# A four-layer graph network: node tiles kept in the order of their edge counts, source rows relabelled on VectorE

## The chip, the cores and the metric

The kernel runs on one core of one Trainium2 chip, as one launch. The metric is the device time of the launch in microseconds (us), smaller being better.

## The reference

A graph has 6250 nodes with 128 features each and 100,000 edges (`src`, `dst`, sorted by `dst`). Four layers are applied, each to `relu(layernorm(x))` and added to `x`:

```python
x = x + L0(h)   # continuous filters: per edge x[dst] * fsum(edge_weight), summed at src; two dense products
x = x + L1(h)   # two graph attention layers, 1 head: softmax over the edges of dst, sum of h[src]
x = x + L2(h)   # per edge MLP on [x[src], edge_attr, global], mean at dst, MLP on the nodes
x = x + L3(h)   # graph attention, 8 heads
```

Layers 1 to 3 gather a row of each edge's source node and sum at the destination node. Layer 0 reads the row of the destination node and sums at the source node. Nothing in the result depends on the order in which nodes or edges are stored, but output row i must be node i.

## The kernel before

Nodes are held on chip in 49 tiles of 128 (the last has 106), which is dimension `b` of `X`, `ACC`, `H`. Edges are sorted into slots, 128 to an edge tile. An edge tile of the regular part (733 tiles, `REG`) holds edges of one destination node tile alone; what is left over, some 49 tiles (`ZT`), lies in "the zone", where an edge tile may touch several node tiles. Eight edge tiles make a half: 92 regular halves and 13 zone halves (`IH`), the latter placed between the regular ones by a table (`Order`; in layer 0 after the halves 5, 10, ..., 65).

**Setup** (L275 to 1034). VectorE counts the edges of each node tile, finds for each node tile where its edges begin (L806 to 827, 21 small instructions in a row, each of which waits for the one before), and then computes a slot for each edge, chunk by chunk of columns (`slot_round`, `slot_rows`). As chunks become ready, GpSimd (POOL) scatters the records (64 attributes and 5 fields) to `edge_records` in DRAM with 782 indirect DMAs (L559), 28 to a round, and ScalarE copies each round's fields and indices (L721, L723). SyncE (SP) loads `x` near the start (L438, L439); VectorE waits for it at L1011, late in setup. ScalarE serves the square root of the first layer norm (L743) only after the copies of round 25.

**Layer 0, destination pass** (`layer0_dst_pass`, L1531 to 1776). For each half:
- VectorE makes one-hot rows (`prepare`, L1611, L1612, one-hot L1451), waiting first for the DMA that stores the one-hots of two halves before;
- TensorE turns them (`turn`, L1717), ScalarE copies them out of PSUM (L1751, L1752), TensorE multiplies them with the rows of `H` (`pick`, L1729);
- VectorE (`finish_regular`) waits until the ring buffer of four halves before has been scattered (L1637, L1639), then for the product, and scales it (L1643, two instructions, in the trace one row "x2");
- POOL scatters the eight tiles to `layer_messages` with eight indirect DMAs (L1765). After half 72 it also scatters the 49 tiles of the zone (L1772).

The order on VectorE is: prepare half k+1, finish half k, prepare half k+2, and so on. The order on TensorE is: turn k+1, pick k, turn k+2, pick k+1. So between two finishes lie, one after the other, VectorE's prepare, TensorE's turn and TensorE's pick. A zone half has a prepare, a turn and a pick of its own but gives POOL nothing to scatter. SP stores the one-hots and the turned ones for the later layers (L1578, L1581) and loads the next half's records (L1572). The record fields of all regular halves stay on chip (`fields`); after the last half two casts (L1703, L1704) make `src_ix`, the gather indices of layers 1 to 3, out of them.

**Layers 1 to 3** each store a table of node rows and gather from it with indirect DMAs on POOL (L1929, eight per half, and 49 for the zone), with TensorE, VectorE and ScalarE working on the halves behind. The destination tile of each edge tile is read from a table (`acc_of_d`, `tile_of_d`, `acc_of_s`) into registers (TENSOR_LOAD, L1458, L1465).

**Output** (L2648 to 2673). VectorE finishes `X` in four parts of 12, 12, 12 and 14 node tiles, and SP writes each part with one DMA (L2670), and the 106 rows of the last tile with another (L2672).

Of the kernel before, what the change touches and what calls it, by code (L numbers as in the profile page):

```python
# [19 lines left out]
I32 = mybir.dt.int32  # L20
# [124 lines left out]
def gnn(nc, a, out):  # L145
# [30 lines left out]
    with ctx:  # L176
# [15 lines left out]
        tile_of_i = sb("tile_of_i", [1, IH * G], I32)  # L192
        adc = sb("adc", [P, NBP * 48], BF16)
# [80 lines left out]

        def setup():  # L275
# [56 lines left out]
            upto = [tb([P, NB2]) for q in range(3)]  # L332
            upto_col = [tb([64, 1]) for q in range(3)]
            edges_upto, before_zone = tb([P, NB2]), tb([P, NB2 + 1])
            zone_from, zone_shift = tb([P, NB2]), tb([P, NB2])
# [19 lines left out]
            with stage_of_work():  # L355
# [19 lines left out]
                masked_ready, slots_summed = sem("masked_ready"), sem("slots_summed")  # L375
                filt_ready, cos_ready, upto_ready, upto_turned, reached_ready, tiles_counted = (
# [28 lines left out]
                with nc.Block() as block:  # L405
                    @block.sync
                    def _(sp):
# [70 lines left out]
                    def _(pool):  # L478
# [17 lines left out]
                        for t in bias_row:  # L496
                            st.then(pool.memset(t[:, D:D + 2], 0.0))
                        pool.sem_inc(consts, 1)
# [74 lines left out]
                    def _(pe):  # L573
# [18 lines left out]
                        for q in range(2):  # L592
                            nc.tensor.matmul(bank[q][:, 0:NB2], tri[0:EP, :], count[q], start=True, stop=True)
                            nc.tensor.matmul(bank[2 + q][:, 0:NB2], ones[0:EP, :], count[q], start=True,
                                             stop=True).then_inc(offs_in_psum, 1)
                        for f in range(FILTERS_AHEAD, NF):
                            add_filter(f)

                        pe.wait_ge(weights_in, 16 * NW)
                        for n, (w, lo, hi) in enumerate(((wm1, 0, 128), (wm1, 128, 192), (wm1, 192, 256))):  # L600
# [7 lines left out]
                        for c in range(1, CHUNKS):  # L608
                            for i in range(NB2):
# [21 lines left out]
                        for q in range(3):  # L631
# [3 lines left out]
                        for q in range(2):  # L635
                            pe.wait_ge(reached_ready, q + 1)
                            for n in range(2):
                                nc.tensor.matmul(bank[2 + n][:, 0:NTP // 2], ones[0:NODE_TILES, :],
                                                 reached[0:NODE_TILES, n * (NTP // 2):(n + 1) * (NTP // 2)],
                                                 start=True, stop=True).then_inc(tiles_counted, 1)  # L640
# [106 lines left out]
                    def _(dve):  # L747
# [58 lines left out]
                        dve.wait_ge(offs_in_psum, 2)  # L806
                        st.then(v.tensor_copy(ntile[0], bank[2][:, 0:NB2]))
                        st.then(v.tensor_scalar(ntile_i[1], bank[3][:, 0:NB2], float(2 * P - 1), None, ALU.add))
                        st.then(v.tensor_copy(ntile_i[0], ntile[0]))
                        st.then(v.tensor_tensor_scan(edges_upto, ntile[0], ntile[0], 0.0, ALU.add, ALU.bypass))  # L810
                        st.then(v.tensor_single_scalar(ntile_i[0], ntile_i[0], 7, ALU.logical_shift_right))
                        st.then(v.tensor_single_scalar(ntile_i[1], ntile_i[1], 8, ALU.logical_shift_right))
                        st.then(v.tensor_tensor(zone_shift, edges_upto, ntile[0], ALU.subtract))
                        st.then(v.tensor_copy(ntile[0], ntile_i[0]))
                        st.then(v.tensor_scalar(ntile[1], ntile_i[1], 2.0, None, ALU.mult))
                        st.then(v.tensor_tensor_scan(upto[0], ntile[0], ntile[0], 0.0, ALU.add, ALU.bypass))
                        st.then(v.tensor_tensor_scan(upto[1], ntile[1], ntile[1], 0.0, ALU.add, ALU.bypass))
                        st.then(v.memset(before_zone[:, 0:1], 0.0))
                        st.then(v.tensor_scalar(upto[0], upto[0], float(REG), None, ALU.min))
                        st.then(v.tensor_tensor(ntile[1], upto[1], ntile[1], ALU.subtract))  # L820
                        st.then(v.tensor_scalar(before_zone[:, 1:NB2 + 1], upto[0], float(P), None, ALU.mult))
                        st.then(v.tensor_scalar(ntile[1], ntile[1], float(P), -1.0, ALU.mult, ALU.add))
                        st.then(v.tensor_copy(zone_from, before_zone[:, 1:NB2 + 1]))
                        st.then(v.scalar_tensor_tensor(off[0], before_zone[:, 0:NB2], -1.0, bank[0][:, 0:NB2], ALU.add, ALU.add))
                        st.then(v.tensor_tensor(off[1], ntile[1], bank[1][:, 0:NB2], ALU.add))
                        st.then(v.tensor_tensor(zone_shift, zone_shift, before_zone[:, 0:NB2], ALU.subtract))
                        st.then(v.scalar_tensor_tensor(zone_shift, zone_shift, float(ZONE_AT * P), zone_from, ALU.add, ALU.subtract))
# [107 lines left out]
                        for c in range(1, CHUNKS):  # L935
                            for i in range(NB2 // 2):
                                slot_round(i, c, loop_c, (c - 1) * (NB2 * 6) + i * 12, False)
                            slot_rows(c, Steps(dve, chunk_steps, c * 13 - 13).then)
                        dve.sem_inc(filter_taken, 1)

                        st.then(v.tensor_tensor(edges_upto, edges_upto, zone_from, ALU.subtract))
# [1753 lines left out]
```

## Time and profile before

| | |
|---|---|
| runs (us) | 6757.25, 6766.14, 6769.0; median 6766.14 |
| profiled execution (us) | 6757.42, of which the span is 6755.7 |
| busy of the span | POOL 70%, PE 50%, VectorE (DVE) 47%, ScalarE (ACT) 23% |
| setup | 0 to about 1209 us |
| layer 0, destination pass | about 1209 to 2220 us |
| output | from 6735 us |

Busy shares are means over stages that have different limits, so each stage is read by itself. The instructions that fill the time are POOL's indirect DMAs: what counts is how long POOL has to wait for the next one to be allowed. PE is TensorE, PEld its weight loads; a name with q at its end (SPq, DVEq) is the engine's own queue, whose DMA issues and register loads aren't counted as busy.

### The profile page before, as it was taken

How to read it: one execution, taken by the hardware profiler on the slowest of the kernel's cores; microseconds unless marked ns; L12 is line 12 of the kernel's file. 1: busy time of each engine (PE TensorE's matmuls, PEld its weight loads, DVE VectorE, ACT ScalarE, POOL GpSimd, SP SyncE). 2: the span in 40 equal slices, each digit the busy share in tenths (PEclk: the TensorE clock that was granted, in tenths of full speed). 3: DMA queues.
4: the chain of work that ended last, by engine and by line, in shares of the span. 5: the costliest groups of instructions: out<-in, count | busy, mean ns of one | idle time of the engine just before them, and what ended most of it. 6: DMA issues, size and time to landing. Idle time of an engine off the chain costs nothing. (4 is left out here: it accounts for less than half of the span.)

```text
span 6755.7 us, 70389 instructions
## 1 busy us (share of the span) xinstructions
PE 3366.4 (50%) x17726; PEld 2923.7 (43%) x17726; DVE 3206.9 (47%) x10050; ACT 1571.4 (23%) x3893; POOL 4738.0 (70%) x4985
## 2 busy tenths in 40 slices
PE   5444301455544773455533455544477776255554
PEld 2222101455543762444432444444476664244443
DVE  8999711333332462333344433336244436465555
ACT  6000000222211671322222322223122224000000
POOL 3677777677777737777756777775777774777775
PEclk8555555667766885666666666666687777566665
DMA  2233333455543744444434444443354542455444
GB/s 73 82 120 118 108 117 104 152 174 173 175 155 134 246 146 122 146 141 145 142 94 123 147 145 142 145 117 117 105 156 145 151 144 73 126 150 145 147 144 117
DMA packets 494348, 913.25 MB, mean 135 GB/s; under 512 B 207337, under 2 KB 242624, under 8 KB 493699
## 3 DMA queue, kind: packets, MB, share of 16 engines
q1 hardware_dynamic: 343814, 617.78, 27.2%
q0 software_dynamic: 150144, 290.98, 16.3%
q8 instruction: 159, 2.61, 0.2%
q14 instruction: 231, 1.89, 0.1%
HBM read 663.11 MB, written 245.25 MB: 134 GB/s over the span
## 5 line engine op out<-in xcount | busy, mean ns | idle before, releaser
L1929 POOL DMA_INDIRECT edge_buf<-node_table,ixr x1472 | 1391.1, 945 | 483.3 <-issue 445.5
L1929 POOL DMA_INDIRECT Y<-node_table,ixr x1460 | 1378.1, 944 | 444.9 <-issue 444.3
L1529 DVE TENSOR_TENSOR ACC<-ACC,bank 128x129 f32 (+3 forms) x3320 | 965.2, 291 | 620.7 <-issue 116.1
L559 POOL DMA_INDIRECT edge_records<-edge_buf x782 | 753.2, 963 | 259.6 <-issue 236.1
L2202 PE MATMUL bank<-adc,turned_buf 128*128 x2199 | 298.2, 194 | 1253.0 <-DVE z L2131 765.3
L2202 PEld LDWEIGHTS bank<-adc,turned_buf 128*128 128x128 bf16 x2199 | 223.0, 102 | 1366.8 <-issue 1318.5
L1503 PE MATMUL bank<-Y 128*128 128x129 f32 (+3 forms) x2920 | 665.0, 418 | 231.3 <-DVE ACC L1529 171.0
L1503 PEld LDWEIGHTS bank<-Y 128*128 128x128 f32 x2920 | 621.3, 320 | 252.7 <-issue 244.2
L1503 PE MATMUL bank<-edge_buf,Y 128*128 128x129 f32 (+3 forms) x2944 | 639.9, 404 | 163.1 <-DVE ACC L1529 95.0
L1503 PEld LDWEIGHTS bank<-edge_buf,Y 128*128 128x128 f32 x2944 | 598.0, 306 | 181.0 <-issue 180.1
L2125 DVE TENSOR_REDUCE pk<-bank 128x16 f32<-128x48 f32 (+1 forms) x276 | 89.1, 323 | 1086.8 <-DMA edge_buf<-node_table,ixr 631.6
L1717 PE MATMUL bank<-ident,Y 128*128 128x128 f32 x840 | 193.2, 405 | 533.8 <-DVE Y L1451 531.5
L1765 POOL DMA_INDIRECT layer_messages<-edge_buf,ixr x368 | 352.5, 958 | 142.4 <-issue 108.4
L611 PE MATMUL bank<-XI,ident 128*128 128x280 f32 (+2 forms) x500 | 279.3, 714 | 325.9 <-DVE XI L877 325.9
L1765 POOL DMA_INDIRECT layer_messages<-Y,ixr x365 | 349.4, 957 | 116.2 <-issue 109.9
L1717 PEld LDWEIGHTS bank<-ident,Y 128*128 128x128 f32 x840 | 152.4, 210 | 556.1 <-DVE Y L1451 553.5
L611 PEld LDWEIGHTS bank<-XI,ident 128*128 128x128 f32 x500 | 146.7, 324 | 457.7 <-DVE XI L877 425.2
L2415 PE MATMUL bank<-wmbT,turned_buf 64*128 64x128 f32 x1584 | 251.0, 320 | 187.1 <-DVE Y L2340 139.3
L1729 PE MATMUL bank<-H,Y 128*128 x1680 | 335.3, 383 | 6.0 <-DVEq L1648 3.2
L1729 PEld LDWEIGHTS bank<-H,Y 128*128 128x128 f32 x1680 | 331.1, 301 | 11.5 <-issue 11.4
L2415 PEld LDWEIGHTS bank<-wmbT,turned_buf 64*128 64x128 f32 x1584 | 228.5, 226 | 214.7 <-DVE Y L2340 150.6
L1751 ACT COPY Y<-bank 128x512 f32<-128x512 f32 x210 | 125.0, 595 | 744.2 <-PE bank L1729 743.6
(400 smaller groups left out, 5786.3 us busy)
## 6 DMA issues: line engine op xcount, KB each, us to landing
Y<-onehots SPq DMA_DIRECT2D x368, 512.0 KB, 3.7
turned_buf<-onehots_turned SPq DMA_DIRECT2D x276, 256.0 KB
layer_messages<-ACC SPq DMA_DIRECT2D x28, 2112.0 KB
edge_buf<-edge_records SPq DMA_DIRECT2D x191, 288.0 KB, 3.3
onehots<-Y SPq DMA_DIRECT2D x105, 512.0 KB, 3.6
XI<-layer_messages SPq DMA_DIRECT2D x84, 528.0 KB, 4.7
onehots_turned<-turned_buf SPq DMA_DIRECT2D x105, 256.0 KB, 2.0
zone_oh<-onehots SPq DMA_DIRECT2D x52, 512.0 KB, 4.0
```

Of the source, the lines that this page charges most:

```text
L559: pool.indirect_dma_start(rec_d, bass.IndirectOffsetOnAxis(ap=ixs[h][:, j:j + 1], axis=0), rec[h][:, j, :], None) \
L611: nc.tensor.matmul(slot_sums(c), ident[0:EP, 0:EP], masked(c, i), start=i == 0, stop=i == NB2 - 1) \
L1503: ins = nc.tensor.matmul(self.places.at(k, j, self.w), tiles_of_half(onehots)[:, j, :], messages[:, j, 0:self.w], start=True, stop=True)
L1529: nc.vector.tensor_tensor(acc, acc, self.places.at(k, j, self.w), ALU.add).then_inc(self.added, 1)
L1717: ins = nc.tensor.transpose(bank[j // 4][:, (j % 4) * P:(j % 4) * P + P], tiles_of_half(oh[k % 2])[:, j, :], ident[:, :])
L1729: ins = nc.tensor.matmul(bank[2 + j // 4][:, (j % 4) * P:(j % 4) * P + P], ohT[k % 2][:, j * P:j * P + P], Hflat[:, bass.ds(at[j] * AW, D) ...
L1751: nc.scalar.copy(ohT[h][:, at], bank[n][:, :]).then_inc(ohT_ready, 1)
L1765: pool.indirect_dma_start(msg_d, bass.IndirectOffsetOnAxis(ap=ixr[r][:, j:j + 1], axis=0), ring[r][:, j, 0:MW], None).then_inc(sent[r], 16)
L1929: pool.indirect_dma_start(ring[q][:, j, 0:w], None, table, bass.IndirectOffsetOnAxis(ap=ixr[q][:, j:j + 1], axis=0)).then_inc(rows_in[q], 16)
L2125: st.then(nc.vector.tensor_reduce(ps, picks(q).rearrange("p (j t k) -> p j k t", j=G, t=3), AX.X, ALU.add))
L2202: ins = nc.tensor.matmul(picks(q)[:, j * 6 * heads:(j + 1) * 6 * heads], ohbT[q][:, j * P:j * P + P], adc[:, bass.ds(at[j] * (6 * heads), ...
L2415: ins = nc.tensor.matmul(bank[2 + j // 4][:, (j % 4) * P:(j % 4) * P + P], attrT[e % 2][:, j * P:j * P + P], wmbT[:, :], start=True, stop= ...
```

## The change

Each full node tile gets a rank by its number of edges (fewest first; the tile of 106 rows stays last), and the node tiles lie in `X`, `ACC`, `H` and in the tables in DRAM in the order of these ranks.

- **Setup, ranks.** Between the counts and the first slots VectorE computes edge counts with ties broken, compares them all with all (`smaller`), and TensorE sums the comparisons (`rank_row`, `rank_col`) and the full edge tiles and remainders of the smaller node tiles, which take the place of the running sums. 42 instructions stand where 21 stood.
- **Setup, loads.** `x` is loaded one node tile at a time: for each, SP reads the tile's first row from `node_at` into a register and issues a DMA. This is done in the scatter rounds 14 to 21, six tiles to a round. The big DMA at the start is gone.
- **Setup, end.** The tables of places are made from five rows where there were three; some dozen small instructions more.
- **Layer 0, destination pass.** The gather indices must name the new rows. `label_sources`, called after each `finish_regular`, computes for a third of the edge tiles at a time `label += (source tile == b) * moved[b]` for b = 0 to 47, two VectorE instructions for each b, four b to a half. The first third is done in the halves 32 to 44, the second in 62 to 74, the last (with the zone) in 78 to 90. After half 64 SP issues 14 more loads of record fields. The two casts after the last half are gone.
- **Output.** One DMA for each node tile, each after a register load of `node_at`, the even ones issued by SP and the odd ones by ScalarE.

The diff, cut to its core:

```diff
@@ setup, SP @@
-                        sp.wait_ge(x_zero, 1)
-                        sp.dma_start(X[:, 0:FULL, :], a["x"][0:FULL * P, :].rearrange("(b p) f -> p b f", p=P)).then_inc(x_in, 16)
-                        sp.dma_start(X[0:REST, FULL, :], a["x"][FULL * P:N, :]).then_inc(x_in, 16)
+                        x_from, x_a_round = EC // (4 * SC), 6
...
+                        def load_x_tile(b):
+                            sp.dma_start(X[:, b, :], a["x"][bass.ds(node_row(mybir.EngineType.SP, b), P), :]).then_inc(x_in, 16)
...
+                            if i == x_from:
+                                load_x()
+                            for b in range((i - x_from) * x_a_round, (i - x_from) * x_a_round + x_a_round):
+                                if 0 <= b < FULL:
+                                    load_x_tile(b)
@@ setup, TensorE @@
+                        pe.wait_ge(sizes_ready, 1)
+                        nc.tensor.matmul(bank[5][:, 64:64 + NB2], full_col[0:NB2, :].to_broadcast([NB2, P]), smaller[0:NB2, :],
+                                         start=True, stop=True)
...
+                        nc.tensor.matmul(bank[4][:, 0:NB2], ones[0:NB2, :], smaller[0:NB2, :], start=True, stop=True)
@@ setup, VectorE @@
+                        st.then(v.tensor_scalar(smaller[0:NB2, :], size_row[0:NB2, :], size_col[0:NB2, :], None, ALU.is_gt))
...
+                        dve.wait_ge(ranks_in_psum, 2)
+                        st.then(v.tensor_copy(rank_row, bank[4][:, 0:NB2]))
+                        st.then(v.tensor_tensor(moved[:, :], rank_row, iota_row[:, 0:NB2], ALU.subtract))
+                        st.then(v.tensor_scalar(moved[:, :], moved[:, :], float(P), None, ALU.mult))
...
-                        dve.wait_ge(x_in, 32)
+                        dve.wait_ge(x_in, 16 * NODE_TILES)
@@ layer0_dst_pass @@
+            late_from, late_loaded_after = 78, 64
+            label_parts = ((0, 31, 32), (31, 62, 62), (62, REG_HALVES, 78))
...
+                        if half == ("regular", late_loaded_after):
+                            for n in range(late_from, REG_HALVES):
+                                sp.dma_start(late_fields[:, (n - late_from) * G:(n - late_from) * G + G, :],
+                                             rec_v[n].rearrange("p (j w) -> p j w", j=G)[:, :, EA:RW]).then_inc(late_in, 16)
...
+                    def label_step(n, step):
...
+                        elif step <= by_rank:
+                            b = step - 1
+                            label_then(v.tensor_scalar(move, key, iota_row[:, b:b + 1], moved[:, b:b + 1], ALU.is_equal, ALU.mult))
+                            label_then(v.tensor_tensor(label[:, 0:count], label[:, 0:count], move, ALU.add))
...
+                    label_steps_each, label_steps_all = 4, by_rank + 2
+
+                    def label_sources(i):
+
+                        for n, (lo, hi, after) in enumerate(label_parts):
+                            first = (i - after) * label_steps_each
+                            for step in range(max(first, 0), min(first + label_steps_each, label_steps_all)):
+                                label_step(n, step)
...
                         (finish_regular if kind == "regular" else finish_zone)(k, i)
+                        if kind == "regular":
+                            label_sources(i)
...
-                    nc.vector.tensor_copy(src_ix[:, 0:ZONE_AT].unsqueeze(2), fields[:, :, R_SRC - EA:R_SRC - EA + 1])
-                    nc.vector.tensor_copy(src_ix[:, ZONE_AT:NT].unsqueeze(2), zone_fields[:, :, R_SRC - EA:R_SRC - EA + 1])
@@ output @@
-                        sp.dma_start(out[tiles.start * P:whole * P, :].rearrange("(b p) f -> p b f", p=P),
-                                     X[:, tiles.start:whole, :]).then_inc(written, 16)
+                        for b in range(tiles.start, min(tiles.stop, FULL), 2):
+                            sp.dma_start(out[bass.ds(node_row(mybir.EngineType.SP, b), P), :], X[:, b, :]).then_inc(written, 16)
...
+                @block.scalar
+                def _(act):
+                    for n, tiles in enumerate(parts):
+                        act.wait_ge(part_ready[n], 1)
+                        for b in range(tiles.start + 1, min(tiles.stop, FULL), 2):
+                            act.dma_start(out[bass.ds(node_row(mybir.EngineType.Activation, b), P), :], X[:, b, :]) \
+                                .then_inc(written_by_act, 16)
```

**Where the label instructions stand.** VectorE in layer 0's destination pass, before, two regular halves in a row (`edge_buf`, `XI`, `Y` are the buffers of records, fields and one-hots; `bank` is PSUM):

```order
L1611 COPY XI<-edge_buf 128x40
L1612 TENSOR_TENSOR XI<-edge_buf,adc 128x8
L1451 TENSOR_TENSOR Y<-bank,XI 128x1024
L1637 COPY edge_buf<-XI 128x8
L1639 CAST ixr_153<-XI 128x8
L1643 TENSOR_TENSOR edge_buf<-bank,XI 128x4x128 x2
L1611 COPY XI<-edge_buf 128x40
```

The same place in the changed kernel, in half 33; the pair of rows L1804 and L1805 stands there four times (shown once):

```order
L1714 COPY XI<-edge_buf 128x40
L1715 TENSOR_TENSOR XI<-edge_buf,adc 128x8
L1542 TENSOR_TENSOR Y<-bank,XI 128x1024
L1740 COPY edge_buf<-XI 128x8
L1742 CAST ixr_161<-XI 128x8
L1746 TENSOR_TENSOR edge_buf<-bank,XI 128x4x128 x2
L1804 TENSOR_SCALAR XI<-XI,iota_row,moved 128x248
L1805 TENSOR_TENSOR bank<-bank,XI 128x248
...
L1714 COPY XI<-edge_buf 128x40
```

Eight instructions now stand between the finish of one half and the prepare of the half after the next.

**The ranks in setup.** VectorE in the changed kernel, right after the last instruction that does not depend on the counts' sums (L856 there, L804 before); before, L807 followed directly:

```order
L856 TENSOR_SCALAR XI<-Y 128x784
L858 TENSOR_SCALAR H<-iota_row 50x50
L859 TENSOR_SCALAR H<-iota_row 50x50
L860 TENSOR_TENSOR H<-H 50x50
L861 TENSOR_TENSOR H<-H,iota_row 50x50
L862 SCALAR_TENSOR_TENSOR H<-H,ident 50x50
L863 TENSOR_REDUCE Y<-H 50x1
L865 SCALAR_TENSOR_TENSOR H<-bank,H 50x50
L866 SCALAR_TENSOR_TENSOR Y<-bank,Y 50x1
L867 CAST Y<-bank 50x1
L868 TENSOR_SCALAR H<-H,Y 50x50
```

Small instructions came in ahead of the first slots; 42 of them now stand between L856 and the first slot round.

**The output on SP's queue.** Before, the last rows of SP:

```order
L2665 UNCONDITIONAL_BRANCH
L2670 DMA out_dram<-X 128x12x128 x4
L2672 DMA out_dram<-X 106x128
L2657 UNCONDITIONAL_BRANCH
...
```

In the changed kernel each node tile has three rows there, and as many on ScalarE's queue:

```order
L2816 UNCONDITIONAL_BRANCH
L279 TENSOR_LOAD node_at
L2821 ISA
L2821 DMA out_dram<-X 128x128
L279 TENSOR_LOAD node_at
...
```

A DMA of 12 tiles became six on each of two queues, each behind a register load.

## Rows read from the trace of the kernel before

**Rows 1.** The page's head and its list of busy time per engine.

```profile
span 6755.7 us, 70389 instructions
...
PE 3366.4 (50%) x17726; PEld 2923.7 (43%) x17726; DVE 3206.9 (47%) x10050; ACT 1571.4 (23%) x3893; POOL 4738.0 (70%) x4985
```

**Rows 2.** One line, L1643: who waited for it (us in all, times).

```profile
  POOL layer_messages L1765: 13.5, 23
```

**Rows 3.** Timeline of POOL, after half 41 and in half 81: start, length, idle before.

```profile
1643.44 0.96 POOL L1765 DMA_INDIRECT layer_messages<-edge_buf,ixr  x1 [0.82 <-DVE edge_buf L1643]
...
2112.61 0.97 POOL L1765 DMA_INDIRECT layer_messages<-edge_buf,ixr  x1 [0.31 <-issue]
```

**Rows 4.** Groups of POOL by line: busy us, mean ns, idle before; the zone's scatter.

```profile
L1772 POOL DMA_INDIRECT layer_messages<-ACC,XI x49 | 46.9, 957 | 14.9 <-issue 14.9
```

**Rows 5.** Timeline of VectorE from the finish of half 38 to that of half 39.

```profile
1605.90 1.29 DVE L1643 TENSOR_TENSOR Y<-bank,XI 128x512 f32<-128x512 f32 x2 [5.33 <-PE bank L1729]
...
1607.62 1.22 DVE L1451 TENSOR_TENSOR Y<-bank,XI 128x1024 f32<-128x1024 f32 x1
...
1613.88 1.29 DVE L1643 TENSOR_TENSOR Y<-bank,XI 128x512 f32<-128x512 f32 x2 [4.83 <-PE bank L1729]
```

**Rows 6.** Timeline of TensorE in the same stretch: turn, then pick.

```profile
1608.90 1.15 PE L1717 MATMUL bank<-ident,Y 128*128 128x128 f32 x8 [3.04 <-DVE Y L1451]
1610.51 3.33 PE L1729 MATMUL bank<-H,Y 128*128 x16 [0.46 <-issue]
```

**Rows 7.** Timeline of VectorE: the finishes of the halves 36, 41, 66 and 72.

```profile
1590.09 1.29 DVE L1643 TENSOR_TENSOR edge_buf<-bank,XI 128x512 f32<-128x512 f32 x2 [4.78 <-PE bank L1729]
...
1641.36 1.29 DVE L1643 TENSOR_TENSOR edge_buf<-bank,XI 128x512 f32<-128x512 f32 x2 [4.71 <-PE bank L1729]
...
1896.99 1.29 DVE L1643 TENSOR_TENSOR Y<-bank,XI 128x512 f32<-128x512 f32 x2 [5.05 <-PE bank L1729]
...
1950.59 1.29 DVE L1643 TENSOR_TENSOR edge_buf<-bank,XI 128x512 f32<-128x512 f32 x2 [5.33 <-PE bank L1729]
```

**Rows 8.** Timeline of VectorE in half 81, the same for all halves from 78 on.

```profile
2083.36 0.18 DVE L1637 COPY edge_buf<-XI 128x8 f32<-128x8 f32 x1 [7.00 <-DMA layer_messages<-edge_buf,ixr]
```

**Rows 9.** Groups and lines of setup that resemble the label instructions (mean or min/median/max ns).

```profile
L867 DVE TENSOR_TENSOR bank<-bank,Y 128x140 f32<-128x140 f32 x150 | 39.1, 306 | 2.6
...
L260 DVE TENSOR_SCALAR H<-X,mean,var x50: 335/340/502, 1093.1 to 1105.6; 128x128 f32<-128x128 f32 x50
...
L988 DVE TENSOR_SCALAR H<-H,Y 50x736 f32<-50x736 f32 x1 | 0.6, 595 | 0.0
...
L991 DVE TENSOR_SCALAR H<-H,Y x1: 267/267/267, 960.2 to 960.2; 50x104 f32<-50x104 f32 x1
```

**Rows 10.** Timeline of VectorE in setup, from the counts' sums to the first slot round.

```profile
70.31 0.21 DVE L807 COPY H<-bank 128x50 f32<-128x50 f32 x1
70.55 0.21 DVE L808 TENSOR_SCALAR H<-bank 128x50 int32<-128x50 f32 x1
...
75.29 0.44 DVE L848 TENSOR_SCALAR Y<-Y,iota_row 128x168 bf16<-128x168 bf16 x2
```

**Rows 11.** Timeline of POOL in setup: the first scatter.

```profile
194.53 1.30 POOL L559 DMA_INDIRECT edge_records<-edge_buf  x1 [9.90 <-ACT edge_buf L723]
```

**Rows 12.** Waits in setup (us in total, times, longest).

```profile
DVE var L254 <- ACT var L743: 107.3, 1, 107.3
```

**Rows 13.** Two stretches of setup: busy us (and instructions) of PE, PEld, DVE, ACT, POOL.

```profile
600.00:700.00 100.00, 46.92 (x80) 23.45 (x80) 94.06 (x287) 2.12 (x12) 74.72 (x79) 0.50 0.30 97
800.00:900.00 100.00, 2.89 (x10) 2.36 (x10) 3.56 (x16) 2.12 (x12) 75.91 (x80) 0.50 0.37 122
```

**Rows 14.** Register loads: one line (min/median/max ns), and the timeline behind one.

```profile
L1458 DVEq TENSOR_LOAD <-acc_of_d x420: 593/596/628, 2551.2 to 6727.4; - x140
...
1616.20 1.15 DVE L1627 TENSOR_TENSOR XI<-XI,adc 128x1 f32<-128x1 f32 x8 [1.03 <-issue]
```

**Rows 15.** Timeline of SP's queue: seven loads of fields, then a store of one-hots; the output.

```profile
1218.66 6.29 SPq L1589 DMA_DIRECT2D XI<-edge_records  x7
1225.07 0.71 SPq L1578 DMA_DIRECT2D onehots<-Y  x1
...
6737.25 12.00 SPq L2670 DMA_DIRECT2D out_dram<-X  x4
...
6749.29 0.52 SPq L2672 DMA_DIRECT2D out_dram<-X  x1
```

More of the change, by code:

```diff
@@ L272, in relu, with node_row @@
             then(v.tensor_scalar(t, t, 0.0, None, ALU.max))
+        def node_row(engine, b):
+            return nc.values_load_multi_w_load_instructions(
+                node_at[0:1, b:b + 1], engines=[engine], min_val=0, max_val=(FULL - 1) * P,
+                skip_runtime_bounds_check_because="setup cuts them at FULL - 1")[1][0]
         def setup():
@@ L331, in setup @@
             ntile_i = [tb([P, NB2], I32) for q in range(2)]
[L332 to L335, printed above, removed]
+            upto = [tb([P, NB2]) for q in range(5)]
+            upto_col = [tb([64, 1]) for q in range(5)]
+            edges_before, edges_here = tb([P, NB2]), tb([P, NB2])
+            zone_from, zone_to, zone_shift = tb([P, NB2]), tb([P, NB2]), tb([P, NB2])
+            tile_col, late_row, late_col = tb([64, 1]), tb([64, NB2]), tb([64, 1])
+            size_row, size_col, smaller, at_rank = tb([64, NB2]), tb([64, 1]), tb([64, NB2]), tb([64, NB2])
+            full_col, full_col_i, rest_col, rank_row, rank_col, rank_step = (
+                tb([64, 1]), tb([64, 1], I32), tb([64, 1]), tb([P, NB2]), tb([64, 1]), tb([64, 1]))
+            passed = tb([64, NTP])
+            less_tile_col = tb([64, 1])
             place_in_zone = tb([1, IH * G])
@@ L630, in _ @@
                         pe.wait_ge(upto_ready, 1)
-                        for q in range(3):
+                        for q in range(5):
                             nc.tensor.transpose(bank[q % 2][0:NB2, q // 2 * P:q // 2 * P + P], upto[q], ident[:, :]) \
@@ L825, in _ @@
                         st.then(v.tensor_tensor(off[1], ntile[1], bank[1][:, 0:NB2], ALU.add))
[L826 to L827 removed]
+                        dve.wait_ge(ranks_in_psum, 1)
+                        st.then(v.tensor_tensor(ntile[0], ntile[0], bank[5][:, 64:64 + NB2], ALU.add))
@@ L1554, in layer0_dst_pass @@
             zone_pos = part(ZT).bitcast(I32)
+            late_from, late_loaded_after = 78, 64
+            late_fields = part((REG_HALVES - late_from) * G * (RW - EA)).rearrange("p (t k) -> p t k", k=RW - EA)
+            label_parts = ((0, 31, 32), (31, 62, 62), (62, REG_HALVES, 78))
+            labels = max(hi - lo for lo, hi, after in label_parts) * G + ZT
+            src_tile, src_move = part(labels), part(labels)
+            label = bank[7][:, 0:labels]
+            by_rank = NODE_TILES - 1
             rec_v = rec_d[0:SLOTS, :].rearrange("(k p j) w -> k p (j w)", p=P, j=G)
@@ new lines, in label_step @@
+                    def label_step(n, step):
+                        v = nc.vector
+                        count = sum(columns.stop - columns.start for columns, rows in label_columns(n))
+                        key, move = src_tile[:, 0:count], src_move[:, 0:count]
+                        if step == 0:
+                            if label_parts[n][1] > late_from:
+                                dve.wait_ge(late_in, 16 * (REG_HALVES - late_from))
+                                dve.wait_ge(zone_in, 16 * ZH)
+                            at = 0
+                            for columns, rows in label_columns(n):
+                                wide = columns.stop - columns.start
+                                here = rows[:, :, R_SRC - EA:R_SRC - EA + 1]
+                                label_then(v.tensor_copy(move[:, at:at + wide].bitcast(I32).unsqueeze(2), here))
+                                label_then(v.tensor_copy(label[:, at:at + wide].unsqueeze(2), here))
+                                at += wide
+                            label_then(v.tensor_single_scalar(move.bitcast(I32), move.bitcast(I32), 7, ALU.logical_shift_right))
+                            label_then(v.tensor_copy(key, move.bitcast(I32)))
+                        elif step <= by_rank:
+                            b = step - 1
+                            label_then(v.tensor_scalar(move, key, iota_row[:, b:b + 1], moved[:, b:b + 1], ALU.is_equal, ALU.mult))
+                            label_then(v.tensor_tensor(label[:, 0:count], label[:, 0:count], move, ALU.add))
+                        else:
+                            at = 0
+                            for columns, rows in label_columns(n):
+                                wide = columns.stop - columns.start
+                                label_then(v.tensor_copy(src_ix[:, columns], label[:, at:at + wide]))
+                                at += wide
```

142 lines of the change are left out of this document (106 added, 36 removed).

## The prediction, made before the run

> **What bounds the kernel now.** I read the page first. POOL is the busiest engine [rows 1], and its time is indirect DMAs, one every 1.26 us (0.96 and 0.30 of issue [rows 3]). A half has eight of them, 10.1 us. So in each stage the question is whether something holds POOL back; work on other engines is free as long as nothing does. The change puts most of its work into layer 0's destination pass, so I looked there for who waits for whom. POOL waited for VectorE's L1643 in 23 places [rows 2], 13.5 us in all. That is little, but it says that the chain behind POOL runs at about POOL's own pace. The timelines show the chain: a finish of 1.29 us, the next one-hot done at 1608.84 (L1451 starts at 1607.62 and takes 1.22) [rows 5], then the turn from 1608.90 and the pick from 1610.51 to 1613.84 [rows 6], and the next finish at 1613.88: 8.0 us, in which TensorE waits for VectorE (3.04) and VectorE for TensorE (4.83). VectorE's idle half isn't spare: it is the other engine's turn. A zone half needs a link of its own and feeds POOL nothing. From finish 36 to finish 41 (five regular halves and a zone half) the chain takes 51.3 us [rows 7], POOL's work for five halves is 50.5, and POOL stands waiting at the end of that stretch [rows 3]. So from half 5 to half 66 the chain has no slack. Behind half 66 no zone halves come: six halves take the chain 53.6 us (1896.99 to 1950.59 [rows 7]) and POOL 60.6. Behind half 72 POOL scatters the zone for 61.8 us [rows 4] and the chain runs ahead until the ring is full; from half 78 VectorE waits 7.00 us in each half for its buffer [rows 8], and half 81 is finished at 2083.5, 29.1 us before its scatter at 2112.61 [rows 3]. POOL needs 2.1 us of that (finish at 1641.36, scatter at 1643.44), so 27 us can be lost there.
>
> **The change part by part.**
>
> *Label instructions, price.* A pair is one TENSOR_SCALAR with two pointer scalars, SBUF to SBUF, and one TENSOR_TENSOR on PSUM and SBUF, 248 columns each. The first: L260 has that form at 128 columns, 0.340; the slope from L991 to L988 is (595 - 267) / 632 = 0.52 ns a column [rows 9], so 0.340 + 120 x 0.00052 = 0.40. The second: L867 has its form at 140 columns, 0.306 [rows 9]; with the one-hot's 1.22 at 1024 columns [rows 5] the slope is 1.04 ns, so 0.42. Between instructions that wait for each other lies 0.03 (L807 to L808 [rows 10]), twice. Together 0.89 us, and four pairs 3.56 us to a half. A third has 48 pairs, 42.7 us, and some 2 us at its ends (four or five casts and copies): 44.7. Bounds: both instructions no longer than their models at 128 and 140 columns, 0.71 a pair; the first at a full column per 1.04 ns, 0.95.
>
> *Label instructions, place.* They stand behind the finish of one half and ahead of the prepare on which the next turn waits, so each adds its full length to the chain, and PE's in-order queue can't pull the pick ahead of the turn. TensorE's gap grows from 3.0 to 6.6 us as well. Its turn and pick took 4.94 us in half 39 [rows 6]; I add 0.3 us a half for a lower granted clock behind longer gaps (0 to 0.6).
> - Halves 32 to 44: no slack, so all of 44.7 + 13 x 0.3 = 48.6 us is POOL's.
> - Halves 62 to 65: the same, 4 x 3.86 and 0.7 for the heavier start: 16.1.
> - The labels of 66 to 71: chain 53.6 + 6 x 3.86 = 76.8 against POOL's 60.6: 16.2. Those behind 72 and 74 lie under the zone's scatter, at nothing; without it they would cost as much a half.
> - Halves 78 to 90 are 289 columns wide, 3.8 a half and 0.4 for the clock: 12.2 against 10.1, 12.5 times 2.1 = 26 us of the 27. Hidden, just; at the high price of a pair some 8 us come out.
>
> Sum 81 us, from 58 (0.71 a pair and no clock loss: 2.84 a half gives 36, 12 and 10) to 104 (0.95 a pair and 0.6: 4.4 a half gives 57, 18, 20 and the 8 above; 0.95 is rounded).
>
> *Loads after half 64.* Seven such loads took SP 6.29 us [rows 15], so 14 take 12.6, and the one-hot store of that half stands behind them. The next but one one-hot waits for that store, some 16 us later. I take 1 us, 0 to 8.
>
> *Setup.* 21 instructions took 75.29 - 70.31 = 4.98 us [rows 10], 0.24 each; 42 take 5.0 more, and the TensorE sums come while VectorE is busy with others. The first scatter waits for the chunk behind them [rows 11], and all rounds follow it: +5 (4 to 8). Everything later on VectorE lies under the 107.3 us that it waits for ScalarE's root [rows 12]; with that cover gone it would cost some 8 us. The `x` loads ride on SP, six to a round of 28 scatters (35 us) at about 1.2 us each; the last are issued in round 21, 194.5 + 21 x 35.3 = 936 us at the earliest, and `x` is wanted shortly before 986 (L260 starts at 1093.1 [rows 9], behind that wait). If they come late, the same 107 us hide it.
>
> *Output.* A register load is 0.60 us, and on VectorE 1.03 passed from the end of one instruction to the start of the next with a load between [rows 14]; a DMA issue is 0.4 us (the small one 0.52 [rows 15]). A node tile costs a queue 0.95 to 1.45, I take 1.2. Four parts of six come every 3.7 us (12.00 us for three [rows 15]), so each queue is behind from the first on and ends at 6737.25 + 24 x 1.2 = 6766.0; with 0.5 for the small tile, 2 of landing and 1.2 of exit 6769.8, 14 us past the span. Bounds +8 and +21. The Trainium skill ("DMA: Bandwidth & Descriptors", Latency and other measured facts) puts the floor of a register load at about 600 ns, and the row agrees. It says as well (Issuing engines are not separate DMA queues) that a second queue saves only issue time; no row here shows that, and issue time is what is scarce at this place.
>
> *The rest.* Gathers and scatters are as many as before and random before and after; one-hots, products and adds are the same. Nothing.
>
> Sum: 81 + 1 + 5 + 14 = 101 us on 6757.4, the profiled execution's own time: 6858. That execution stands 9 us below the median of the runs; I put 6860.
>
> **The rivals.**
> - *The label work is mostly hidden* (faster instructions than modelled, or slack in the chain that I overlooked): what speaks for it is that VectorE stands idle for 4.83 us of each 8.0; against it, that this idle stretch ends with TensorE's result [rows 5] and TensorE's with VectorE's [rows 6]. With a third of the 81 us: 6757 + 27 + 20 = 6804.
> - *POOL is held up by VectorE's label instructions.* If each SBUF-to-SBUF instruction kept POOL from writing descriptors for its length, the third stretch would no longer be hidden (48 x 0.42 = 20 us) and the 27 us of lead would be spent too: 6858 + 20 and up, 6885. Setup speaks against it: with VectorE at 94% POOL does 79 scatters in 100 us, with VectorE at 4% it does 80 [rows 13]. This is the warning of the Trainium skill ("SBUF — State Buffer", SBUF: two separate sides) that a VectorE instruction in a two-port mode locks GpSimd out of descriptor writing; by these rows it doesn't bite here.
> - *Faster: rows in another order make the indirect DMAs cheaper.* There are six times 782 of them; each would have to lose 101 / 4692 = 22 ns of its 1.26 us before the kernel gains anything. Setup's scatters (edges by destination) and layer 0's (places by source) address quite different rows, and both come every 1.26 us (79 to 80 in 100 us [rows 13]; 0.96 and 0.30 [rows 3]), so the order of rows doesn't show in them. At 30 ns it would be 6858 - 141 = 6717.
> - *No change:* label work hidden whole, output and setup at their low bounds: 6757.4 + 8 + 4 = 6769, just inside 0.2%.
>
> **How the numbers follow.** Forecast 0.76 (6815 to 6900), mostly hidden 0.10 (6785 to 6815), POOL held up 0.07 (above 6880), same 0.04, faster 0.03. A measurement of this kernel tells 0.2% (13.5 us) from no change. Slower is the sum of the first three, 0.93. The range leaves out what is below 6800 and above 6905.
>
> **What would show it.** In the destination pass POOL's waits for L1746 should be about 81 us where they were 13.5, none of it before half 32; finishes in the halves 33 to 44 should be 11 to 12 us apart where they were 8.0, with POOL waiting in each; from 78 to 91 no wait on POOL, and the lead shrinking from 29 to a few us. The pair L1804, L1805 should take 0.89 us. The first scatter should come at about 199.5. SP's last output issue should be at about the last part's readiness plus 17 us. The prediction is wrong if the finishes stay 8 us apart with labels in them, if POOL's pace leaves 1.26 us, or if register loads on SP run well below 0.6 us.

## The result and the profile after

The changed kernel takes 6849.98 us (median of 4 runs, 6842.36 to 6858.56), the kernel before 6765.86 (4 runs). The ratio is 1.0123, 95% interval 1.011 to 1.0135: slower by 84 us. The forecast was 6860 with a range of 6800 to 6905. The profiled execution took 6842.36 us, 84.9 over that of before.

The head of the page and the busy time show little: VectorE works 139 us more, POOL 1 us more [rows 1].

```profile
span 6840.4 us, 71218 instructions
...
PE 3349.6 (49%) x17750; PEld 2906.3 (42%) x17750; DVE 3346.1 (49%) x10390; ACT 1571.5 (23%) x3893; POOL 4739.2 (69%) x4986
```

The finish is now L1746. Who waited for it (us in all, times): POOL 88.7 us in 42 places, where it was 13.5 in 23 [rows 2] and I had put about 81.

```profile
  POOL layer_messages L1916: 88.7, 42
  DVE XI L1730: 9.8, 9
  DVE XI L1804: 1.1, 7
```

VectorE's timeline from one finish to the next, inside the first third. Four pairs of label instructions (1644.53 to 1648.24) stand ahead of the prepare, whose one-hot L1542 is what TensorE's turn waits for.

```profile
1643.09 1.29 DVE L1746 TENSOR_TENSOR Y<-bank,XI 128x512 f32<-128x512 f32 x2 [4.19 <-PE bank L1880]
1644.53 0.41 DVE L1804 TENSOR_SCALAR XI<-XI,iota_row,moved 128x248 f32<-128x248 f32 x1
1644.97 0.42 DVE L1805 TENSOR_TENSOR bank<-bank,XI 128x248 f32<-128x248 f32 x1
...
1650.31 1.23 DVE L1542 TENSOR_TENSOR Y<-bank,XI 128x1024 f32<-128x1024 f32 x1
...
1656.29 1.29 DVE L1746 TENSOR_TENSOR edge_buf<-bank,XI 128x512 f32<-128x512 f32 x2 [4.60 <-PE bank L1880]
```

The finishes are 13.2 us apart here (the step with a register load in it; 11 to 12 us without, and 20.7 and 22.6 around a zone half). POOL's timeline has the other side: a first scatter after a long wait (the longest of the halves with labels, behind a zone half), the rest back to back. The last two lines are VectorE's finish of half 90, in the last third, and POOL's first scatter of that half, 4.9 us later.

```profile
1680.99 0.95 POOL L1916 DMA_INDIRECT layer_messages<-edge_buf,ixr  x1 [12.82 <-DVE edge_buf L1746]
1682.24 0.96 POOL L1916 DMA_INDIRECT layer_messages<-edge_buf,ixr  x1 [0.31 <-issue]
...
2276.41 1.29 DVE L1746 TENSOR_TENSOR Y<-bank,XI 128x512 f32<-128x512 f32 x2 [5.32 <-PE bank L1880]
...
2281.34 0.96 POOL L1916 DMA_INDIRECT layer_messages<-Y,ixr  x1 [0.30 <-issue]
```

TensorE in the same stretch [rows 6]: its gap grew to 6.67 us. Turn and pick end 5.4 us after their start in this half, but over the halves of the first third (1550 to 1740 us) they take 4.74 us on average, where they took 4.83 before.

```profile
1662.93 1.97 PE L1868 MATMUL bank<-ident,Y 128*128 128x128 f32 x8 [6.67 <-DVE Y L1542]
1664.69 3.62 PE L1880 MATMUL bank<-H,Y 128*128 x16
```

The finishes of the halves 66 and 72, the same two as at the end of [rows 7]:

```profile
1960.38 1.29 DVE L1746 TENSOR_TENSOR Y<-bank,XI 128x512 f32<-128x512 f32 x2 [4.32 <-PE bank L1880]
...
2035.00 1.29 DVE L1746 TENSOR_TENSOR edge_buf<-bank,XI 128x512 f32<-128x512 f32 x2 [4.68 <-PE bank L1880]
```

They are 74.6 us apart (53.6 before). Read as delays of each half's first scatter against the trace of before, the whole 84.7 us by which the span grew (the time beside it grew 0.2) comes apart so:

| stretch | delay at its start, at its end (us) | added | predicted |
|---|---|---|---|
| setup and the halves up to 32 | 0, 4.5 | 4.5 | 5 |
| halves 32 to 46 (first third) | 4.5, 49.1 | 44.6 | 48.6 |
| halves 62 to 66 | 48.8, 63.4 | 14.6 | 16.1, and 1 for loads |
| halves 66 to 73 | 63.4, 77.3 | 13.9 | 16.2 |
| halves 73 to 91 (last third) | 77.3, 77.7 | 0.4 | 0 |
| up to the end of the last gather | 77.7, 79.5 | 1.8 | 0 |
| output and end | 79.5, 84.7 | 5.2 | 14 |

The first scatter of setup was 4.7 us late (199.22 against 194.53 [rows 11]), and the first of the destination pass 6.4, of which 1.9 were won back by half 32 in POOL's small waits (0.3 more between the halves 46 and 62). How much is won back differs from one execution to the next: in the other kernels with the same setup the delay at half 32 was between 2.9 and 7.4 us. The lead of the finish over its scatter was 29.3 us at half 78 and 4.9 at half 90. VectorE's label instructions by line (min, median, max in ns):

```profile
L1804 DVE TENSOR_SCALAR XI<-XI,iota_row,moved x144: 408/411/634, 1554.1 to 2277.8; 128x248 f32<-128x248 f32 x96, 128x289 f32<-128x289 f32 x48
...
L1805 DVE TENSOR_TENSOR bank<-bank,XI x144: 423/425/468, 1554.6 to 2278.3; 128x248 f32<-128x248 f32 x96, 128x289 f32<-128x289 f32 x48
```

The output in SP's and ScalarE's queues, 24 register loads and DMAs on each [rows 15], and the register loads by line:

```profile
6817.30 19.02 SPq L2821 DMA_DIRECT2D out_dram<-X  x24
6836.37 0.32 SPq L2822 DMA_DIRECT2D out_dram<-X  x1
...
6817.28 19.45 ACTq L2830 DMA_DIRECT2D out_dram<-X  x24
...
L279 SPq TENSOR_LOAD <-node_at x72: 262/272/525, 704.3 to 6835.5; - x72
L279 ACTq TENSOR_LOAD <-node_at x24: 272/282/475, 6816.6 to 6835.9; - x24
```

A tile costs each queue 0.81 us (19.45 / 24): 0.28 is the register load, 0.35 the DMA's issue, the rest register arithmetic.

### The profile page after: what moved, and what is told of

It is laid out like the page before. It is cut to its first block and busy times, and to the rows that moved or that the text cites. A ratio compares the mean times of both kernels' runs of the same rounds, so it can differ in the third digit from the quotient of the medians.

```text
span 6840.4 us, 71218 instructions
## 1 busy us (share of the span) xinstructions
PE 3349.6 (49%) x17750; PEld 2906.3 (42%) x17750; DVE 3346.1 (49%) x10390; ACT 1571.5 (23%) x3893; POOL 4739.2 (69%) x4986
```

## The experiments

Theory: the label instructions cost time only because they stand between a finish and the prepare, in the chain that feeds POOL; the same instructions are free wherever POOL or VectorE's own wait covers them. Rivals: VectorE's instructions hold POOL up, and the order of rows changes the price of the indirect DMAs. The kernel before was run beside each call: medians 6759.3 us (first four kernels), 6761.6 (next three) and 6767.4 (last four). A single run is the profiled execution, and is compared with that of the change, 6842.36 us.

### Labels ahead of the finish

```diff
                         if k + 1 < len(order.halves):
                             prepare(k + 1)
-                        (finish_regular if kind == "regular" else finish_zone)(k, i)
                         if kind == "regular":
                             label_sources(i)
+                        (finish_regular if kind == "regular" else finish_zone)(k, i)
```

> The label steps of a regular half stand ahead of its finish instead of behind it: the same instructions, as many and as long, but in the 4.8 us in which VectorE waits for TensorE's turn and pick. Mine (they cost only because they stand in the chain turn, pick, finish, one-hot that feeds POOL): finishes in halves 33 to 44 come 8 us apart again, POOL's 89 us of waits for the finish fall back to 13 to 20, and the kernel takes 6850 - 73 = 6777, 6770 to 6785. Rival (VectorE's extra instructions between SBUF and SBUF hold up POOL's descriptor work, wherever they stand): no gain, 6845 to 6855. Rival (the destination pass is longer because of the order of rows in the tables): no gain either.

Measured: 6771.07 us (10 runs), ratio 1.0017, 95% 1.0008 to 1.0027, so 12 us over before, and 72 less than the change's own 84. VectorE's timeline shows the same eight instructions at the same lengths, now in its wait for the pick, of which 0.91 us are left:

```profile
1611.16 1.29 DVE L1746 TENSOR_TENSOR Y<-bank,XI 128x512 f32<-128x512 f32 x2 [1.65 <-PE bank L1880]
...
1612.89 1.23 DVE L1542 TENSOR_TENSOR Y<-bank,XI 128x1024 f32<-128x1024 f32 x1
1614.03 0.40 DVE L1804 TENSOR_SCALAR XI<-XI,iota_row,moved 128x248 f32<-128x248 f32 x1
...
1617.26 0.42 DVE L1805 TENSOR_TENSOR bank<-bank,XI 128x248 f32<-128x248 f32 x1
...
1618.87 1.29 DVE L1746 TENSOR_TENSOR Y<-bank,XI 128x512 f32<-128x512 f32 x2 [0.91 <-PE bank L1880]
```

The finishes are 7.7 us apart, and POOL waits for them no more than in the kernel before:

```profile
  POOL layer_messages L1916: 12.4, 28
```

The delay against before is 5.4 us at half 32 and 5.3 at half 72. Both rivals fall: neither where the rows lie nor that VectorE works in that time costs anything that a run of this size would show. Of the 14.7 us by which this profiled execution is over that of before, 5.8 are there at the last scatter and 5.2 in the output; the other 3.7 came in the gather passes, where nothing was edited.

### No labels in the first two thirds, or in the last

```diff
-                        elif step <= by_rank:
+                        elif step <= by_rank and n < 2:
+                            pass
+                        elif step <= by_rank:
```

(The other kernel has `n == 2` in that line.)

> The 2 x 48 pairs of the first two thirds are left out (their source labels stay without the part that moves them, so later gathers fetch other rows of the same tables). Mine: both thirds' 73 us come off, destination pass about 73 us shorter, 6770 to 6782; with the labels moved ahead of the finish the same, within 3 us. Rival (part of the 73 us is something else than the label instructions, the row order or setup's shift): less than 60 us come off.

> The 48 pairs of the last third alone are left out (their source labels stay unmoved, as above). Mine: those 50.5 us of VectorE's work lay under the 29 us of lead that the finishes have over their scatters, so nothing comes off: 6840 to 6852, and the lead at half 90 stays near 29 us where it fell to 4.9. Rival (VectorE's SBUF-to-SBUF instructions hold up POOL): 48 x 0.42 = 20 us off, 6822 to 6830.

Measured: 6771.65 us without the first two, 6844.49 without the last (one run each). The first gives 71 us (72 by the medians beside it), and equals the kernel above with its labels in place (6771.07): hidden costs what left out costs. The last gives nothing. Its finish of half 90 stands 29.1 us ahead of its scatter:

```profile
2250.92 1.28 DVE L1746 TENSOR_TENSOR Y<-bank,XI 128x512 f32<-128x512 f32 x2
...
2280.02 0.96 POOL L1918 DMA_INDIRECT layer_messages<-Y,ixr  x1 [0.30 <-issue]
```

### One more instruction to a pair in the last third

```diff
-label_then(v.tensor_scalar(move, key, ...))
+for again in range(2 if n == 2 else 1):
+    label_then(v.tensor_scalar(move, key, ...))
```

> In the last third each pair's first instruction is issued twice, 48 x (0.41 + 0.03) = 21 us more of VectorE's work in halves 78 to 90. Mine: the third was hidden under a lead that fell from 29.3 to 4.9 us and can't fall under 2.1, so 2.8 of the 21 us are hidden and 18 come out: 6842 + 18 = 6860, 6856 to 6865. Rival (that stretch has other slack, or POOL's queue covers more): 6850 or less.

Measured: 6872.95 us (one run), 13 over the expectation. The mechanism is there: between half 78 and half 90 the delay against before goes from 84.0 to 102.4 us, 18.4 where I expected 18; the lead falls from 29.5 us at half 78 to 2.2 at half 85, and from half 86 on POOL waits, about 3.5 us in each half. POOL's group in the stretch 2140 to 2300 us, and the first scatter of half 90:

```profile
L1917 POOL DMA_INDIRECT layer_messages<-edge_buf,ixr x62 | 60.6, 977 | 24.1 <-issue 18.3 <-DVE edge_buf L1746 5.9
...
2306.02 1.09 POOL L1917 DMA_INDIRECT layer_messages<-Y,ixr  x1 [3.62 <-DVE Y L1746]
```

The other 13 us are spread over the program: 6 us of them are there at half 72, and 6.5 come in the gather passes, where nothing was edited. POOL's own pace was slower in this execution (see the last section).

### Ranks by number

```diff
-size_row, bank[2], 64.0, late_row, ALU.mult, ALU.add
+size_row, bank[2],  0.0, late_row, ALU.mult, ALU.add
```

(and the same for `size_col`)

> The sizes by which the tiles are ranked are multiplied by 0, so that every tile keeps its number's place: the same instructions on every engine, but rows in the tables in the old order. Mine (order of rows costs and gives nothing): 6850 within 5 us, POOL's pace 1.26 us in every stage. Rival (ordered rows make the indirect DMAs cheaper or dearer and hide part of the label work's price or add to it): a change in all six passes, of at least 13 us in all.

Measured: 6844.95 us (4 runs), ratio 1.0128, 95% 1.0111 to 1.0145, where the change itself has 1.0123. The order of the rows neither costs nor gives anything that can be told. POOL does 79 scatters in the stretch 600 to 700 us, as before [rows 13] (columns: stretch, its length, PE, PEld, DVE, ACT and POOL busy with instructions, granted clock, DMA share, GB/s):

```profile
600.00:700.00 100.00, 46.33 (x80) 23.47 (x80) 94.00 (x290) 1.77 (x10) 74.74 (x79) 0.50 0.34 112
```

### Setup made longer

```diff
+for again in range(21):
+    st.then(v.tensor_scalar(moved[:, :], moved[:, :], 1.0, None, ALU.mult))
```

> 21 more dependent small VectorE instructions (each a multiplication by 1 on the 128 x 48 row of rank moves) in setup, behind the ranks. Mine: 21 x 0.24 = 5.0 us; first scatter at 204 where it was 199.2, and all stages by 5 us later, but half 32 by 4 us or less; 6844 to 6850 on the profiled run's 6842. Rival (setup is not on the path there, the 4.7 us came from TensorE's sums): first scatter stays at 199.2.

Measured: 6846.84 us (one run). The first scatter comes at 203.91, 4.69 us after that of the change (199.22), 0.22 us for each of the 21; at half 32 the delay is 9.4 us where it was 4.5, so all of it was still there, where I had expected 4 us or less. Small dependent instructions in that chunk are on the path to the end, at their full length.

```profile
203.91 1.30 POOL L588 DMA_INDIRECT edge_records<-edge_buf  x1 [9.89 <-ACT edge_buf L775]
```

### The output, four ways

One load of all the row registers of a part, put ahead of the wait for that part:

```diff
+at = node_rows(SP, tiles, 0)
 sp.wait_ge(part_ready[n], 1)
-    sp.dma_start(out[bass.ds(node_row(SP, b), P), :], ...)
+    sp.dma_start(out[bass.ds(at[b - tiles.start], P), :], ...)
```

> The registers with the output rows of a part's tiles are loaded ahead of the wait for that part, not one ahead of each output DMA. After this change the output costs 5 us past the last gather, 0.81 us a tile on each queue. Mine: what is left of it is half register loads (0.27 us each), half DMA issue (0.54): the queues keep step with the parts (six tiles every 3.7 us at 3 x 0.54 = 1.6 a queue), and the end comes 2 to 5 us earlier: 6845 to 6848. Rival (the queues were not behind, and the 5 us are the small parts' own order of work or landing): no gain, 6850.

Measured: 6844.94 us (4 runs), ratio 1.0122. The time is about the one I expected, but the ratio is the change's own: no gain. From the last gather's end to the end of the span 41.3 us pass (41.9 in the change, 36.7 before). The edit fetched a register for every tile of the part, twice what a queue uses, and a queue works in order, so the load for part 2 stood behind the issues of part 1, at 0.8 to 2.9 us:

```profile
L279 SPq TENSOR_LOAD <-node_at x4: 769/988/1121, 6812.9 to 6831.2; - x4
L279 ACTq TENSOR_LOAD <-node_at x4: 2608/2734/2883, 6812.9 to 6834.9; - x4
```

The loads moved, they did not go. This and the labels ahead of the finish in one kernel:

> Labels ahead of the finish and output rows' registers read ahead, together. Mine: the two gains add up: 6850 - 73 - 4 = 6773, that is 4 to 12 us above the kernel before. Rival (the gains overlap or one of them isn't there): 6777 or more.

Measured: 6772.80 us (median of 10 runs), ratio 1.0017, 95% 1.0008 to 1.0026, the same as with the labels alone. An eleventh run took 12651.18 us; its cause isn't known, and it is left out here. The number fits, its working doesn't: there was no second gain to add.

All 24 registers of a queue, only its own, loaded ahead of the first wait:

```diff
+at = node_rows(SP, 0)          # node_at[0:1, 0:FULL:2]
 for n, tiles in enumerate(parts):
     sp.wait_ge(part_ready[n], 1)
-        sp.dma_start(out[bass.ds(node_row(SP, b), P), :], ...)
+        sp.dma_start(out[bass.ds(at[b // 2], P), :], ...)
```

> All 24 row registers of each queue are loaded ahead of the wait for the first part. In the run before, with one load of several registers per part, it stood behind the issues of the part before and took 0.8 to 2.9 us; now it lies in the wait. Mine: issue alone is 0.52 us a tile, 3.1 for a queue's six in the 3.7 between parts, so the queues keep step with VectorE: from the last gather to the end 37 to 38 us, 4 to 5 less than 41.9; 6840. Rival (the transfers' own pace or their number is what is late): 41 us or more, 6845.

> Tiles keep their numbers' places (sizes multiplied by 0) and the output is written by the four large DMAs of the kernel before. Mine: the 5 us of the output are the small DMAs' issue, so from the last gather to the end of the span it is 36.7 us again where it was 41.9, and the profiled run takes 6837 to 6840. Rival (the wait for a later part or landing does it): 41 us or more.

Measured: 6847.68 us (4 runs, ratio 1.0117, 95% 1.0101 to 1.0132) with the registers up front, 6838.02 (one run) with the four fixed DMAs. I had expected 6840 for the first and 6845 if the rival held, so its total missed, and doesn't tell it from the change; the trace does. Its last gather ends at 6809.39, 10.8 us later than the change's (POOL's pace again, see the last section), and its span at 6846.5, so 37.1 us where it was 41.9. With fixed DMAs it is 6799.69 to 6836.3, 36.6 us. Registers up front, then fixed output (POOL's last gather, then SP's queue):

```profile
6808.44 0.95 POOL L2086 DMA_INDIRECT Y<-node_table,ixr  x1 [0.30 <-issue]
...
6827.78 14.89 SPq L2828 DMA_DIRECT2D out_dram<-X  x24
6842.73 0.33 SPq L2829 DMA_DIRECT2D out_dram<-X  x1
```

```profile
6798.75 0.94 POOL L2080 DMA_INDIRECT Y<-node_table,ixr  x1 [0.30 <-issue]
...
6817.79 12.00 SPq L2821 DMA_DIRECT2D out_dram<-X  x4
6829.83 0.64 SPq L2823 DMA_DIRECT2D out_dram<-X  x1
```

So the output's cost is the time that the register loads take between the issues; the number of DMAs as such costs 0.5 us at most (37.1 against 36.6, and 36.6 in the next kernel, which has the small DMAs too).

### The two that help, together

> Labels ahead of the finish, and all row registers up front. Mine: 6771 - 4.5 = 6766.5, about 5 us over the kernel before, which is setup's share, within 0.2% of it. Rival (no gain from the registers): 6771 to 6773.

Measured: 6773.5 us (11 runs) against 6767.41, ratio 1.001, 95% 1.0001 to 1.0019. It lies within 0.2% of the kernel before and 6 us over it, where I had expected 5; the expected 6766.5 is missed, and the kernel before was itself slower in this call (6767.4, 6759.3 beside the labels alone). The interval of the labels alone (1.0008 to 1.0027) overlaps with this one, so that the registers' gain is in the total is not shown; in its trace it is (from the last gather at 6722.5 to the end of the span at 6759.1, 36.6 us). No version here beats the kernel before. In this trace the first scatter of setup is 4.7 us late, the last gather 3.5 and the end of the span 3.4: what stays is what setup costs, and no version that was run pays it back.

## Why the prediction was right, point by point

- **The chain has no slack from half 5 to half 66: right.** Finishes went from 8.0 to 11 to 13 us apart from the first half with labels on, and putting the labels elsewhere gave back 72 us, nearly all that the two thirds had cost (44.6 + 14.6 + 13.9 = 73.1).
- **The price of a pair: right.** 0.41 + 0.42 us and two gaps of 0.03 to 0.04: 3.62 us for four pairs where I had 3.56.
- **The clock term: wrong.** "I add 0.3 us a half for a lower granted clock behind longer gaps" is 23 x 0.3 = 6.9 us of the sum. TensorE's gap did grow, to 6.5 us, but turn and pick took 4.74 us (4.83 before). Without this term the three stretches come to 44.7, 14.9 and 14.4 against 44.6, 14.6 and 13.9. It is 6.9 of the 7.8 us by which the label part is off.
- **Halves 78 to 90 hidden, "just": right.** 24.4 of the 29.3 us of lead were used. With 21 us more, the lead ran out at half 85, and what came out was the difference (18.4).
- **Loads after half 64: +1, about right.** The halves 62 to 66 added 14.6 us, which the labels alone explain (14.9 without the clock). Where the labels are out of the way, the wait that I named is seen: VectorE's next but one one-hot stands 0.53 us for the one-hot store with the labels ahead of the finish, at no loss, and 0.90 in the run with the output edit as well, where POOL lost 2.8 us at half 66. The wait is 0.4 us longer there than in the former; the rest of the 2.8 lies in longer steps from finish 63 to 66 (9.6, 10.7 and 17.2 us, where they were 8.0, 10.0 and 16.6), whose cause isn't shown. So no wait of more than 0.9 us was seen for the loads, and in the change itself none.
- **Setup +5: right.** 4.7 at the first scatter, 4.5 at half 32.
- **Output +14: too much by 9, the largest miss.** The failed step is "A register load is 0.60 us ... I take 1.2". The 0.596 us of [rows 14] was a load of eight registers, on VectorE; a load of one register on SP and ScalarE is 0.27 to 0.28 us, and a tile costs 0.81. Loads on SP well below 0.6 us were one of the prediction's own signs of being wrong, and for this term they were. So a queue was busy for 19.5 us behind the first part's readiness where SP was for 12.5, 7 us more; and from the last issue's end to the end of the span it is 3.7 us with DMAs of 64 KB (I had 3.2, for which no row stood), where it was 5.9 with 768 KB. Together 5. The Trainium skill ("DMA: Bandwidth & Descriptors", Latency and other measured facts) has about 600 ns as the floor of a register load; the rows of both queues are less than half of that, and here the measurement decides.
- **The rivals.** Mostly hidden: it is what happens if the labels are moved by one line, not where the change puts them. Order of rows: none. POOL held up by VectorE: almost none. In the last third the mean scatter took 962 and 960 ns in the change, 957 without the labels and 977 to 982 with the doubled instruction (973 without those scatters that follow a wait, which took up to 1087, and some 3 of it are that execution's slower pace). For the change that is some 125 x 4 ns = 0.5 us, where the rival had 20. What the Trainium skill warns of ("SBUF — State Buffer", SBUF: two separate sides) shows here, if at all, as these few ns; what makes them isn't shown.
- **The sum.** Predicted 101 on 6757.4; measured 84.9. Of the 16 us between them 7 are the clock term, 9 the output and 1 each the loads and the rest of the labels, less 1.8 us in the gather passes, which no edit touches.

POOL's group in the last third (2134 to 2297 us) of the change: all of its idle time is its own issue.

```profile
L1916 POOL DMA_INDIRECT layer_messages<-edge_buf,ixr x64 | 61.5, 962 | 19.5 <-issue 19.5
```

## What to carry to other kernels

Where two engines take turns, the idle time of one is not spare by itself: an instruction is free only if it is put between the engine's last hand-over and the result it waits for. Here one line moved was worth 72 of 84 us. Before work is added, write down for each stretch who leads whom and by how much; a lead is a stock that can be spent once (29.3 us, of which 24.4 went), and behind it each us counts in full. And take the duration of a small instruction from one of its own size, on the queue that will issue it.

## What the runs showed that I had not expected

- A register load has no one price. In `kernel.py` the load of [rows 14] fetches eight words in one instruction (0.59 us; TensorE's loads of eight take 0.59 too), the one of `acc_of_s` fetches 16 (1.10 us on VectorE), and a load of one word took 0.27 us on SP and 0.28 on ScalarE. So the number of words goes with the time on VectorE alone, and it can explain why SP's loads were shorter; no run has a load of one word on VectorE, so whether the engine matters as well is open. Where the words lie seems to matter too: the 12 consecutive words of a part took 0.8 to 1.1 us on SP, but 11 that begin one word later 2.6 to 2.9 on ScalarE, and 24, every second word, 5.06 us on SP and 5.23 on ScalarE, 0.21 to 0.22 each. Whether the engine or the place of the first word makes the difference between the first two isn't settled. The lines, from the change and from the kernel with the registers up front:

```profile
L2032 DVEq TENSOR_LOAD <-acc_of_s x28: 1096/1101/1122, 2307.6 to 2519.8; - x28
```

```profile
L279 SPq TENSOR_LOAD <-node_at x1: 5057/5057/5057, 6820.9 to 6820.9; - x1
L279 ACTq TENSOR_LOAD <-node_at x1: 5225/5225/5225, 6820.9 to 6820.9; - x1
```

- Executions differ by POOL's pace. The mean setup scatter took 964 ns in the change and 966 in the run with the doubled instruction; the median from one setup scatter to the next is 1.263 us in the former and 1.266 in the latter, and in the gather passes 1.249 and 1.252. The kernel with the registers up front was at 1.266 and 1.252 too. With 4,692 of them that is some 14 us, about as much as single runs of one kernel lie apart (6842 to 6859). The two lines, one of each trace:

```profile
L588 POOL DMA_INDIRECT edge_records<-edge_buf x782 | 753.6, 964 | 259.8 <-issue 238.2
```

```profile
L588 POOL DMA_INDIRECT edge_records<-edge_buf x782 | 755.8, 966 | 258.8 <-issue 239.2
```

- TensorE's gap of 6.5 us instead of 3.8 in each half brought no slower turn and pick. From finish 36 to finish 41 the mean granted clock was 0.70 before and 0.64 in the change (a mean of stretches at 1.2 and at 2.4 GHz); since the same work took as long, I read the lower mean as that of the gaps, which no run here tests.
